# Norms of a slot matrix by a round trip through DRAM, and attention output made token-major: one change to a fused attention and soft-mixture kernel

## The reference

```python
# attention
q = apply_axial_rope(LN(x) @ Wq, pos);  k, v = split(ctx @ Wkv);  k = apply_axial_rope(k, pos)
w = softmax(einsum('bqhd,bkhd->bhqk', q, k) / sqrt(8))
x = x + einsum('bhqk,bkhd->bqhd', w, v).reshape(b, n, 256) @ Wout + bout
# soft mixture
x_n  = l2norm(x_ln, -1) * scale
mu_n = mu / max(sqrt(sum(mu * mu, axis=0)), 1e-12)      # one norm per slot, over the 256 features
logits = einsum('bnd,des->bnes', x_n, mu_n)
dispatch, combine = softmax over n, softmax over all 2048 slots
slot_in = einsum('bnd,bnes->besd', x_ln, dispatch)
h = gelu(slot_in @ W1 + b1);  slot_out = h @ W2 + b2
x = x + einsum('bsd,bns->bnd', slot_out, combine)
```

## Time and profile before

| | |
|---|---|
| median of 3 runs | 533.65 us (533.04 to 535.34) |
| the profiled execution | 533.35 us, of which 531.2 us is its span (first to last instruction) |
| busy: PE, PEld, DVE, ACT, POOL | 475.6, 379.4, 373.2, 303.0, 147.4 us |
| mean granted TensorE clock | 0.974 of full |
| last chain, by engine | PE 60%, DVE 24%, ACT 8%, issue 5% |
| attention and tail | 0 to 240 us |
| mixture steps | 240 to 531 us, PE busy 284.0 of 291.0 us |

### The profile page before, as it was taken

One profiled execution on the slowest core, in us unless ns is written; L12 is line 12 of the kernel. 1 busy time (PEld: TensorE's weight loads), 2 busy tenths in 40 slices (PEclk: granted clock), 3 DMA queues, 4 the chain that ended last, 5 costly groups with the idle time before them and its releaser, 6 DMA issues.

```text
span 531.2 us, 14914 instructions
## 1 busy us (share of the span) xinstructions
PE 475.6 (90%) x5784; PEld 379.4 (71%) x5784; DVE 373.2 (70%) x861; ACT 303.0 (57%) x599; POOL 147.4 (28%) x248
## 2 busy tenths in 40 slices
PE   0768899888988887979999999999999999999995
PEld 0545666654566555658888888888888888888884
DVE  5788999884999889764856576575657565765653
ACT  1346655664655665526468547745764585477454
POOL 3419411334864832302212211211121122112100
PEclk9859999998999999997999999999999999999999
DMA  6600000004200200000000000000000000000000
GB/s 167 239 7 6 7 7 7 7 2 90 85 6 5 68 0 2 3 1 1 11 1 12 12 11 0 10 10 10 0 10 10 0 10 10 10 0 10 11 12 11
DMA packets 15731, 11.71 MB, mean 22 GB/s; under 512 B 7072, under 2 KB 15184, under 8 KB 15440
## 3 DMA queue, kind: packets, MB, share of 16 engines
q1 hardware_dynamic: 15696, 11.21, 7.1%
HBM read 9.11 MB, written 2.10 MB: 21 GB/s over the span
## 4 chain that ended last, share of the span: by engine, by line
PE 60%; DVE 24%; ACT 8%; issue 5%; SPq 1%; DMA 1%; DVEq 1%; ACTq 0%; POOL 0%
PE psum L943 13%; PE psum L944 12%; PE psum L945 12%; PE psum L1166 9%; PE psum L1181 6%; DVE mx L694 5%; DVE rc L711 4%; DVE pb L699 3%; ACT vb L493 3%; PE psum L1022 2%; DVE pb L858 2%; DVE xT_l L663 2%; DVE ra L670 1%; DVE qkr L681 1%; ACT mu_raw L561 1%
## 5 line engine op out<-in xcount | busy, mean ns | idle before, releaser
L561 ACT COPY mu_raw<-psum 128x384 f32<-128x384 f32 x96 | 41.0, 445 | 116.2 <-PE psum L1166 116.2
L836 DVE TENSOR_REDUCE es<-eb 128x4 f32<-128x512 f32 x64 | 42.9, 686 | 61.2 <-ACT eb L553 61.2
L476 ACT ACTIVATE pb<-pb 128x512 f32<-128x512 f32 x64 | 39.3, 631 | 74.1 <-DVE pb L699 74.1
L1166 PE MATMUL psum<-w_raw,eb 64*128 64x129 f32 x1024 | 68.5, 285 | 2.9 <-DVE w_raw L829 1.9
L1166 PEld LDWEIGHTS psum<-w_raw,eb 64*128 64x128 f32 x1024 | 62.6, 193 | 8.2 <-DVE pb L858 3.9
L346 POOL TENSOR_TENSOR sm<-sm,mhalf 128x1 f32<-128x1 f32 x16 | 8.8, 551 | 169.9 <-DVE sm L815 169.9
L943 PE MATMUL psum<-mun_h,xlT_l 128*128 128x512 f32 x128 | 52.3, 408 | 0.2 <-DVE xlT_l L822 0.2
L1008 PE MATMUL psum<-ident,pb 128*128 128x128 f32 x256 | 42.2, 290 | 10.8 <-ACT vb L493 7.8
L858 DVE TENSOR_TENSOR pb<-psum,rh 128x384 f32<-128x384 f32 x96 | 49.2, 513 | 3.3
L1008 PEld LDWEIGHTS psum<-ident,pb 128*128 128x128 f32 x256 | 28.2, 145 | 32.0 <-issue 26.3
L944 PE MATMUL psum<-mun_l,xlT_h 128*128 128x512 f32 x128 | 50.6, 395 | 0.0
(11 more groups left out here) (160 smaller groups left out, 1083.9 us busy)
## 6 DMA issues: line engine op xcount, KB each, us to landing
mu_raw<-in_L_ffn_mu SPq DMA_DIRECT2D x1, 2048.0 KB, 13.3
out<-w_raw SPq DMA_DIRECT2D x16, 128.0 KB, 1.7
xa<-in_x SPq DMA_DIRECT2D x1, 1536.0 KB, 9.2
ctile<-in_ctx SPq DMA_DIRECT2D x16, 64.0 KB, 1.8
w_raw<-in_L_ffn_W SPq DMA_DIRECT2D x2, 512.0 KB, 5.3
w_raw<-in_L_ffn_W SPq DMA_DIRECT2D x1, 1024.0 KB, 9.0
xa<-in_x SPq DMA_DIRECT2D x1, 512.0 KB, 3.4
mu_raw<-in_L_ffn_b SPq DMA_DIRECT2D x1, 512.0 KB, 3.2
```

What stands on the lines that cost most here:

```text
L561: a.copy(eT[:, e0:e0 + n, :].rearrange("p n (b k) -> p b n k", b=2), pair(i, n)[:, :, :, HC:XC]).then_inc(eT_ready, 1)
L1166: m = mm(bank[HB[i % 3] + b][:, n * XC:(n + 1) * XC], eb[rows, e, :], xw[rows, e, :], start=True, stop=True)
```

## The change

Two things are changed together. The inverse norms no longer go through `diag`, PE and ACT: SP writes the 128 by 16 values to a scratch tensor in DRAM, waits, and reads them back as one row into all partitions (`mu_rb`), slots outside and experts inside, and POOL reads them with a permuted pattern. SP does this ahead of the loads of `W1` and `W2` and of the context tiles from 10 on.

And `attend` is turned round: `pT` is now the weight operand (128 rows by 64 columns), and per pair of heads 18 columns of `vb` stream through it, 16 of values and two that hold ones. Its output has tokens as rows, and one sum per head. `normalise` takes 32 reciprocals and multiplies them out into `on`; two PE transposes (`transpose_o`) put `on` into `bank[5]`, and an ACT copy (`oT_copy`) makes `oT` of it. `mu_sums` moves ahead in PE's step and the clamp of the norms moves behind the second `softmax` in DVE's step 6. In the tail, `attend(15)` now stands ahead of `project_out(14)`.

```diff
 # SP
-            sp.wait_ge(rb_filled, 4)
+            sp.wait_ge(mur_ready, 1)
+            sp.dma_start(mur_d, mu_r[:, 1, :]).then_inc(mur_stored, 16)
+            sp.wait_ge(mur_stored, 16)
+            sp.dma_start(mu_rb, row(mur_d.rearrange("s e -> (s e)"), ES)).then_inc(rb_loaded, 16)
 # POOL
-            pool.wait_ge(mur_ready, 1)
-            g.tensor_tensor(diag, ident[:].unsqueeze(1).broadcast_to([P, EXPERTS, P]),
-                            R[1].unsqueeze(2).broadcast_to([P, EXPERTS, P]), ALU.mult).then_inc(diag_ready, 1)
-            pool.wait_ge(rb_ready, 4)
+            pool.wait_ge(rb_loaded, 16)
...
-                g.tensor_tensor(mu_raw[:, k, :], mu_raw[:, k, :], mu_rb, ALU.mult).then_inc(muscale_step, 1)
+                mu_k = mu_raw[:, k, :].rearrange("p (e s) -> p e s", s=SLOTS)
+                g.tensor_tensor(mu_k, mu_k, mu_rb.rearrange("p (s e) -> p e s", e=EXPERTS), ALU.mult)\
+                    .then_inc(muscale_step, 1)
 # ACT
+            def oT_copy(t):
+                act.wait_ge(oT_filled, t + 1)
+                wait(act, a_filled, t)
+                a.copy(oT[:], bank[5][:, 0:DIM]).then_inc(oT_ready, 1)
...
-                        for gr in (g0, g0 + 1):
-                            pT_copy(s - 1, gr)
+                        pT_copy(s - 1, g0)
+                        if out and g0:
+                            oT_copy(s - 2)
+                        pT_copy(s - 1, g0 + 1)
...
-            for c in range(4):
-                act.wait_ge(rb_filled, c + 1)
-                a.copy(mu_rb[:, c * BANK:(c + 1) * BANK], bank[NB[c]][:]).then_inc(rb_ready, 1)
...
+            oT_copy(TILES - 2)
+            oT_copy(TILES - 1)
             sumsq(1, 1)
 # DVE
-                v.reciprocal(rc[:], bank[4][:, DIM:2 * DIM]).then_inc(rc_done, 1)
+                src = bank[4][:, 0:HEADS // 2 * VC].rearrange("p (q c) -> p q c", c=VC)
+                v.reciprocal(rc[:].rearrange("p (q j) -> p q j", j=2), src[:, :, 2 * HD:VC]).then_inc(rc_done, 1)
                 dve.wait_ge(rc_done, t + 1)
-                v.tensor_tensor(oT[:], bank[4][:, 0:DIM], rc[:], ALU.mult).then_inc(oT_ready, 1)
+                wait(dve, oT_filled, t)
+                v.tensor_tensor(on[:].rearrange("p (q j d) -> p q j d", j=2, d=HD),
+                                src[:, :, 0:2 * HD].rearrange("p q (j d) -> p q j d", j=2),
+                                rc[:].rearrange("p (q j) -> p q j", j=2).unsqueeze(3).broadcast_to(
+                                    [P, HEADS // 2, 2, HD]), ALU.mult).then_inc(on_ready, 1)
...
+                softmax(s, p, 2)
                 if norms:
                     dve.wait_ge(muss_ready, 1)
+                    dve.wait_ge(oT_ready, s - 1)
                     v.tensor_scalar(mu_r[:, 0, :], bank[5][:, DIM:DIM + EXPERTS], L2_EPS * L2_EPS, None, ALU.max)\
                         .then_inc(muss_clamped, 1)
-                softmax(s, p, 2)
 # PE, attend
-                for half in range(2):
+                for q in range(HEADS // 2):
+                    i = 4 * (q % 8 // 2) + 2 * (q // 8) + q % 2
                     for b in range(2):
-                        for r in range(2):
-                            for g in range(GROUPS):
-                                c = 256 * r + 32 * (half * GROUPS + g)
-                                product(half, r, g, vb[:, p, b].rearrange("p r c -> p (r c)")[:, c:c + 32],
-                                        slice(64 * b, 64 * b + 64), half * P + b * 64)
-                    for r in range(2):
-                        for g in range(GROUPS):
-                            m = product(half, r, g, hone[:, r, :], slice(0, P), DIM + half * P)
+                        rows = slice(64 * b, 64 * b + 64)
+                        m = mm(bank[4][rows, q * VC:(q + 1) * VC], pT[:, i, rows], vb[:, p, b, q, :],
+                               start=True, stop=True)
                 m.then_inc(o_filled, 1)
+
+            def transpose_o(t):
+
+                pe.wait_ge(on_ready, t + 1)
+                wait(pe, x1_ready, t)
+                for k in range(KD):
+                    m = nc.tensor.transpose(bank[5][:, k * P:(k + 1) * P], on[:, k * P:(k + 1) * P], ident[:])
+                m.then_inc(oT_filled, 1)
 # PE, before step 8
-            for c in range(4):
...
-                mm(bank[NB[c]][:], ones[:], diag[:, 4 * c:4 * c + 4, :].rearrange("p e s -> p (e s)"),
-                   start=True, stop=True).then_inc(rb_filled, 1)
-            pe.wait_ge(rb_ready, 4)
```

More of the change, by code:

```diff
@@ L36 @@
 XC = HC + SEQ
+VC = 2 * HD + 2
 def wait(eng, sem, value):
@@ L233, in build @@
         out_d = out.rearrange("b s d -> (b s) d").rearrange("(t p) d -> p t d", p=P)
+        mur_d = nc.dram_tensor("mur_scratch", (P, EXPERTS), F32, kind="Internal").ap()
         def row(v, n):
@@ L507, in xT_high, with step @@
                 a.copy(flat(xT[0]), bank[7][:, 0:3 * P]).then_inc(xT_split, 1)
-            def step(s, p, before=True, after=True, ahead=True):
+            def oT_copy(t):
+                act.wait_ge(oT_filled, t + 1)
+                wait(act, a_filled, t)
+                a.copy(oT[:], bank[5][:, 0:DIM]).then_inc(oT_ready, 1)
+            def step(s, p, before=True, after=True, out=True, ahead=True):
                 for g0 in (0, 2):
                     if before:
-                        for gr in (g0, g0 + 1):
-                            pT_copy(s - 1, gr)
+                        pT_copy(s - 1, g0)
+                        if out and g0:
+                            oT_copy(s - 2)
+                        pT_copy(s - 1, g0 + 1)
                     for gr in (g0, g0 + 1):
@@ L530, in _ @@
             step(0, 0, before=False)
-            step(1, 1)
-            with act.Fori(1, 4) as i:
-                for p in range(2):
-                    step(i * 2 + p, p)
-            for c in range(4):
-                act.wait_ge(rb_filled, c + 1)
-                a.copy(mu_rb[:, c * BANK:(c + 1) * BANK], bank[NB[c]][:]).then_inc(rb_ready, 1)
-            with act.Fori(4, TILES // 2 - 1) as i:
+            step(1, 1, out=False)
+            with act.Fori(1, TILES // 2 - 1) as i:
                 for p in range(2):
@@ L604, in _ @@
             v.memset(vb[:].rearrange("p a b c d -> p (a b c d)"), 0.0).then_inc(consts_dve, 1)
[L605 to L611 removed]
+            dve.wait_ge(consts_dve, 1)
+            for j in range(2):
+                ones_j = vb[64 * j:64 * j + 64].rearrange("p a b c d -> p (a b c) d")[:, :, 2 * HD + j:2 * HD + j + 1]
+                v.memset(ones_j, 1.0).then_inc(consts_dve, 1)
             def moments(st, L, t0, t1, var_scale, var_bias, step, base, done):
@@ L958, in project_qk @@
                 pe.wait_ge(xT_ready, t + 1)
-                wait(pe, oT_ready, t - 2)
+                wait(pe, on_ready, t - 2)
                 for k in range(KD):
@@ L1040, in project_out @@
                     pe.wait_ge(oT_ready, t + 1)
-                    wait(pe, x1_ready, t)
                 m = mm(bank[b][:, 0:DIM], oT[:, k * P:(k + 1) * P], wo[:, k, :], start=(k == 0), stop=(k == KD - 1))
@@ L1068, in step @@
                     transpose_p(s - 1, 1 - p, 2)
+                if norms is not None:
+                    mu_sums(s, norms)
+                if out:
+                    transpose_o(s - 2)
                 if after and before:
@@ L1071, in step @@
                 logits(s, 2, 0)
-                if norms is not None:
-                    mu_sums(s, norms)
                 if before:
@@ L1215, in _ @@
                 transpose_p(TILES - 1, 1, gr, more=False)
+            transpose_o(TILES - 2)
+            attend(TILES - 1, 1, roped=False)
             for k in range(KD):
                 project_out(TILES - 2, k)
-            attend(TILES - 1, 1, roped=False)
-            pe.wait_ge(x1_ready, TILES - 1)
             pe.wait_ge(w12_ready, 2)
             expand(0)
+            transpose_o(TILES - 1)
             pe.wait_ge(b2_ready, 1)
             pe.wait_ge(e_ready, 4)
+            transpose_xl(1, 1)
             for k in range(KD):
                 project_out(TILES - 1, k)
-            transpose_xl(1, 1)
             ffn_step(0, 0, first=True)
```

44 lines of the change are left out of this document (12 added, 32 removed).

## The result

Ten runs of the changed kernel have a median of 532.42 us (529.45 to 533.25), ten of the kernel before beside them 534.29 (533.04 to 536.09). The ratio is 0.995, 95% interval 0.9928 to 0.9971. By the medians the change gains 1.9 and 3.2 us, by the ratios 2.7 and 4.1, and 4.7 (0.9%, a ratio of 0.991) were forecast. The first interval excludes the forecast ratio, the second does not. So the time lies in the forecast range and the direction is right, but the gain is smaller than forecast: the nearest single figure is about 3 us, and by the median of the first ten runs less than half of the forecast.

What follows compares the result with a forecast made beforehand. Ordinary steps hung on DVE, PE about half a microsecond behind. Terms -4.8 - 7.5 + 2.4 + 2.2 + 0.4 + 2.6 = -4.7 from 533.35 gave 528.65, stated as 528.6 us; range 523.5 to 534.5.

Steps and rivals of the forecast that it cites:

- Reciprocal: In normalise on DVE: 32 columns instead of 256 cost about 0.35 us instead of 1.75, DVE 1.4 us faster.
- attend: On PE: 64 loads at 30 ns, 1.95 us in all and 2.15 to the start of v_copy, as long as before.
- ordinary steps: Attention steps 2, 7 and 9 to 14: each goes from 11.95 to 11.35 us, -4.8 us in all.
- the ring: Chain of one ordinary attention step, from xT_low to the next xT_low: 12.0 us before, closing at 11.35 after.
- DVE's way: DVE's path through an ordinary step: down 0.9 to 11.1 us, leaving PE's way longer by 0.25.
- Serial loads: Rival in attend, chance 0.08: loads not overlapped, attend at 3.9 us, whole kernel 558 us, slower than before.
- Steps 3 to 5: Attention steps that already hang on PE: sums only move, transposes fill the wait, attend costs the same; 0 us.
- Step 8 and the round trip: Norm spread leaves PE and ACT: step 8 from 18.9 to 11.35 us, -7.5; DRAM trip taken as covered, 0.
- Step 6: project_out(4) waits for the clamp now behind two maxima and subtractions, +2.4 us; PE's clock falls to 0.50, +2.2 us.
- The tail: After the last attention step: project_out(14) behind attend(15) makes residual(14) start 3.1 later; project_out(15) and mixture +2.6 us.
- step 15: attend(14) waits for the last pT_copy, which stands behind one more oT_copy: +0.4 us.
- The likeliest case: Whole kernel as summed, 526.5 to 531 us, chance 0.42.

Runs made afterwards that it cites:

- e6_copy_early: Changed kernel with ScalarE's oT copy moved ahead of the exponentials: 527.20 us, ratio 0.9875 to the kernel before.
- e3_norms_only: Kernel before with only the DRAM round trip of the slot norms added, attention output left feature-major: 526.93 us, ratio 0.9874 to the kernel before.
- e2_step6_busy: Changed kernel with ten extra 128x128 identity products on TensorE in step 6 ahead of project_out: 526.28 us, ratio 0.9859 to the kernel before.
- e5_tail_order: Changed kernel with project_out of tile 14 back ahead of attend of tile 15 in the tail: 528.23 us, ratio 0.9893 to the kernel before.
- e10_all_and_64: Changed kernel with clamp ahead of softmax, project_out(14) ahead of attend(15), oT copy ahead of exponentials, and attend streaming 64 columns: 518.10 us, ratio 0.9677 to before.
- e4_attend_only: Changed kernel with the old spreading of the norms, so only the token-major attend half: 535.98 us, ratio 1.0033 to the kernel before.
- e1_clamp_early: Changed kernel with VectorE's clamp of the slot norms ahead of the softmax: 529.81 us, ratio 0.9816 to the kernel before.
- e7_all_three: Changed kernel with clamp ahead of softmax, project_out(14) ahead of attend(15), and oT copy ahead of exponentials, 18 columns: 526.19 us, ratio 0.9817 to the kernel before.
- e9_again: Changed kernel, unedited, timed a second time: 531.32 us, ratio 0.9924 to the kernel before.
- e11_attend_64_again: Changed kernel with attend streaming 64 columns per product instead of 18, timed again: 527.72 us, ratio 0.9858 to the kernel before.
- e12_clamp_64: Changed kernel with the clamp ahead of the softmax and attend streaming 64 columns: 522.51 us, ratio 0.9766 to the kernel before.

## Why the prediction was half right

**Bound and method: right.** The distances of reciprocals gave the right stages, and six of the seven rows of the table came within 1.3 us of their measure. The seventh is off by 3.1.

**Reciprocal, attend, ordinary steps: right.** 0.35 us; 64 loads in 2.0 us, from the row of `combine`; steps of 11.36 to 11.42 against 11.35. The way over `attend` closes the ring, as forecast, though with a wait of 0.37 for `oT_copy` ahead of `project_out` in it, and DVE's way is hardly shorter: with the wait gone (`e6_copy_early`) a step loses only 0.09, not 0.37. Serial loads would have made `attend` 3.9 us, an estimate of the forecast from its rows; these loads share their rows and came every 31 ns, with 18 and with 64 columns streamed. The Trainium skill (TensorE: Matmul & The Clock Gate, Part 3, "The mechanism") says that a load overlaps running matmuls only when its row group differs, beside naming a background weight buffer as another way; this trace does not agree with the row group as the only way.

**Steps 3 to 5: mis-sized.** I said 0, they gave 0.31 each. From a reciprocal's start to the next `project_out`, PE now needs 89.80 - 83.93 = 5.87 us where it needed 90.30 - 84.05 = 6.25. Why it is shorter is not shown; perhaps the transposes fill less than the old wait for `oT`. No run splits this further.

**Step 8 and the round trip: right.** -7.5, and `e3_norms_only` shows it alone, 6.7 us under before. The 3 MB took 13.3 us from the issue of the row, just under my 14 to 17; at 9.0 us for each MB it would have been 27. The transfers also began earlier than I had said, 4.7 us ahead of step 7 (the store at 108.86, the reciprocal at 113.60).

**Step 6: right in both parts.** 2.2 of wait (forecast 2.4) and 3.0 of clock (forecast 2.2), which `e2_step6_busy` separates.

**The tail: the step that failed.** I summed +0.4 for step 15 and +2.6 for the tail, at full clock. Together they measured +6.1, in the changed kernel's first profile and in its second. With the clock up it is +3.4, so the two terms together were sized about right. Their parts were not: the order of the tail, for which I had 3.1, is worth 1.7 (`e5_tail_order`, and the 15.89 - 14.19 of the last kernels); the `oT_copy` in step 15, for which I had 0.4 and named a wait for `pT_copy`, is worth 0.8 (`e6_copy_early`); and 0.9 is left in `e10_all_and_64`, where both are mended. That these errors nearly cancel is luck. What I left out is the clock: I asked what an idle PE does to it in step 6 and nowhere else. In step 15 PE stood 1.43 us for the copy, the clock fell to 0.50, `attend(14)` took 3.00 instead of 2.05 us and the first slot logits ran slow. This is the 2.7 between +3.4 and +6.1. That the wait for the copy is what brings the fall is not shown: the same wait went without a fall in `e2_step6_busy` and `e4_attend_only`, and `e1_clamp_early` and `e7_all_three` had the fall without this wait.

**The clock over the whole kernel: not in the sum at all.** In the last mixture step PE waited 1.44 us for the same copy as before, yet its 64 products (L1177) took 3.68 us at a clock of 0.50, where before they took 2.08. From the products ahead of them (L1162, 512.99; before L1166, 515.07) to the end of the span it is 18.2 us against 16.1. These 2.1 are more than the whole +1.3 of the mixture, and I had no term for them. The changed kernel's 22 runs have mean clocks of 0.955 to 0.971, and streaming 64 columns lifts them to 0.968 to 0.980 and lowers the median by 3.6 us. So the narrow `attend` cost at least as much as the forecast missed. That the edit to 64 columns is what brings the gain is shown by one pair timed side by side (`e9_again` and `e11_attend_64_again`) and borne out by two pairs from different sets, each beside the kernel before (`e7_all_three` and `e10_all_and_64`, whose intervals lie apart, and `e1_clamp_early` and `e12_clamp_64`, whose intervals overlap). How the wider stream keeps the clock up is not shown, and it is not the only way: `e2_step6_busy`, with 18 columns, has clocks of 0.977 or more in five of six runs. In which stage a given run pays is not forecast by anything that I measured.

The likeliest case had the right mechanism in the stages that it looked at and too narrow a range, 526.5 to 531. None of the rivals was a clock that falls in stages behind step 6.

## What to carry to other kernels

Split a joint change before judging it: here one half was worth 6.7 us and the other cost 1.8, and the whole gained less than the first half alone. When a change makes PE wait, or makes its matmuls narrower, ask for the clock in every stage and not only behind the longest wait. And where runs of one kernel spread by 2%, sort them by granted clock before reading the median: the spread of `e1_clamp_early` and `e7_all_three` hid the 5 us that step 6 had gained, and with 64 columns the same edits came to 522.51 and 518.10 us.

## What was unexpected in the hardware

More columns in flight made the kernel faster while no instruction got shorter: `attend` takes 2.05 us with 18 and with 64 streamed columns, and the median fell from 531.32 to 527.72 us, with the clock falling in fewer places. The same wait (1.42 or 1.43 us ahead of `project_out(13)`) was followed by a clock of 0.50 in three profiles (the changed kernel's two and `e5_tail_order`) and by 1.00 in `e2_step6_busy` and `e4_attend_only`, also with 18 columns, and a fall made step 15 longer by 1.2 us at times, by 5.0 at others. So in step 15 an idle stretch of PE does not decide the fall alone.
